# Mixing two batches ahead, a sum without turned rows, and expert weights kept in SBUF

## The chip, the core and the metric

The kernel runs on one core of one Trainium2 chip. The metric is device time in microseconds, as the median of several runs. The core's engines are TensorE (PE, with its weight loads as PEld), VectorE (DVE), ScalarE (ACT), GpSimd (POOL) and SyncE (SP), which here issues only DMAs. The engines run their own instruction streams and meet by semaphores. SBUF is the working memory, PSUM holds the products of TensorE, and DRAM holds inputs, outputs and rows that are dispatched by index.

## What is computed

A decoder of four layers on x (4 batches of 512 rows, 128 wide, fp32) with a context of 77 rows a batch. Each of twelve blocks is `x = layernorm(x + block(x))`. The change touches three of them:

```python
# layer 0, third block: mixing
x_prev = rows of x shifted down by one
xr = mu_r * x + (1 - mu_r) * x_prev
xk = mu_k * x + (1 - mu_k) * x_prev
out = sigmoid(xr @ W_r.T) * (square(relu(xk @ W_k.T)) @ W_v.T)

# layer 1, second block: sum with the context's mean
out = x1 @ W1.T + mean over the 77 rows of (x2 @ W2.T) + b

# layer 3, third block: experts (8 experts, each row goes to its best 2)
shared = (silu(x @ sw1) * (x @ sw3)) @ sw2
rw, sel = top_k(x @ router_w.T + experts_bias, 2);  rw = softmax(rw)
out = shared + sum over the 2 chosen e of rw * ((silu(x @ w1[e]) * (x @ w3[e])) @ w2[e])
```

## The kernel before

The twelve blocks run as a chain of stages. `Core.stage` opens a block of the five engines' streams; its end is a barrier, so no engine begins a stage before all have ended the one before. X holds the rows in their natural order, R the sums before the norm, and XT the rows turned (features on partitions), which most stages need as an operand of TensorE. The norm of a batch is written in four steps that several stages share: `norm_stats` on VectorE adds the block's result to X and takes mean and variance (L122, L125, L128), `norm_gpsimd` takes the power -1/2 on GpSimd (L160, L162) in two halves of a batch, `norm_apply` on VectorE scales into X (L143), and `norm_tensor` with `norm_scalar` turns X on TensorE (L170) and copies it into XT on ScalarE (L177).

**Mixing stage, `mixing_ffn`.** Per batch b of four: ScalarE makes two scaled copies of the shifted rows (`scale`, L1553), VectorE adds mu times x to them (`mix`, L1584 and L1588), TensorE multiplies (`first`, L1512 for k and L1517 for r), ScalarE takes relu and sigmoid (L1563, L1567), VectorE squares the relu (L1598), TensorE multiplies again (`second`, L1526), and VectorE forms the gated product Y (L1603). All buffers have two slots. The order on every engine is written by hand: `scale`, `mix` and `first` run one batch ahead, and `norm_apply` and the turning of batch b - 1 stand within batch b.

**Context stage, `context_sum`.** VectorE sums the context's rows (L1649) and spreads the mean of each batch over 128 columns (L1652). TensorE adds three products for each of 16 groups of rows (L1628 to L1630). The norm follows, and at the end X is turned into XT. The stage that follows, `experts_one`, normalises X once more and turns the result into XT on its own.

**Last stage, `experts_two`.** SyncE first writes X to rows in DRAM (L2907). TensorE and VectorE compute the routing; VectorE then makes a table `expert_i` that holds for each of 39 tiles of 128 rows the expert's number times 128, and the lists of row numbers. GpSimd issues for each tile an indirect gather of its rows into XG (L331, eight slots) and an indirect scatter of its results out of O (L335, four slots): first eight gathers, then for each tile a scatter and, while there are tiles left, a gather. TensorE turns a tile's rows (`turn`, L2951), multiplies with the expert's w1 and w3 (`up`, L2959) and w2 (`down`, L2967). ScalarE copies the turned rows (`take`, L3034) and applies silu (`gate`, L3040); VectorE forms the product (L3108) and copies the result into O (L3114). The orders are by hand: TensorE runs turn(i + 2), up(i + 1), down(i); ScalarE runs gate(i), take(i + 2). The shared expert's work is strewn between the tiles (L2931, L2932, L2943, L3028, L3075, L3080). The weights of a tile's expert, 128 x 768 fp32, are read from DRAM for every tile into WB (four slots) by SyncE:

```python
sp.wait_ge(found, 1)
for i in range(T):
    e = sp.value_load(disp.expert_i[0:1, i:i + 1], min_val=0, max_val=7 * P)
    if i >= RING:
        sp.wait_ge(o_ready, i - RING + 1)
    sp.dma_start(WB[:, i % RING, :], weights[bass.ds(e, P), :]).then_inc(loaded[i % RING], 16)
```

After the loop the results are read back, weighted, added and normalised, and written to the output.

## Time and profile before

| | |
|---|---|
| median of 3 runs | 2083.51 us (2081.59 to 2091.36) |
| profiled execution, its own time | 2109.39 us |
| span of its profile | 2107.5 us |
| PE busy | 1716.1 us (81%) |
| DVE busy | 1422.6 us (68%) |
| ACT busy | 1075.5 us (51%) |
| POOL busy | 416.6 us (20%) |
| granted PE clock, mean | 0.916 |
| DMA | 132.29 MB, mean 63 GB/s |

Times are microseconds from the start of the span unless marked ns. L1512 is line 1512 of the kernel. In a row of a timeline the first number is the start, the second the time covered, then engine, line, operation, output and inputs with their shapes, the count, and in brackets the idle time of the engine before it with what ended it. A row of several instructions covers them with the gaps between. The chain of waits is followed back from the last instruction; a piece named "another core or an unknown queue" is one for which the profile shows no releaser. Ends of matmuls are modelled.

### The profile page before, as it was taken

How to read it: one execution, taken by the hardware profiler on the slowest of the kernel's cores; microseconds unless marked ns; L12 is line 12 of the kernel's file. 1: busy time of each engine (PE TensorE's matmuls, PEld its weight loads, DVE VectorE, ACT ScalarE, POOL GpSimd, SP SyncE). 2: the span in 40 equal slices, each digit the busy share in tenths (PEclk: the TensorE clock that was granted, in tenths of full speed). 3: DMA queues.
4: the chain of work that ended last, by engine and by line, in shares of the span. 5: the costliest groups of instructions: out<-in, count | busy, mean ns of one | idle time of the engine just before them, and what ended most of it. 6: DMA issues, size and time to landing. Idle time of an engine off the chain costs nothing. (4 is left out here: it accounts for less than half of the span.)

```text
span 2107.5 us, 33370 instructions
## 1 busy us (share of the span) xinstructions
PE 1716.1 (81%) x11732; PEld 1022.0 (48%) x11822; DVE 1422.6 (68%) x3275; ACT 1075.5 (51%) x2294; POOL 416.6 (20%) x576
## 2 busy tenths in 40 slices
PE   4779858999977999985789999973699988796773
PEld 3546533333365666663644444432345444464662
DVE  4546578888764776765666767767699999575224
ACT  3346526777723445444455565543477777463221
POOL 0110030000032666652200000001200000100654
PEclk8999889999978999997999999995699999997896
DMA  4000000000025888861000000000000000001454
GB/s 121 1 1 2 1 1 0 1 1 1 1 94 199 315 327 324 334 238 42 1 1 0 1 1 1 1 1 18 1 1 2 2 1 1 1 2 51 136 156 129
DMA packets 42862, 132.29 MB, mean 63 GB/s; under 512 B 7106, under 2 KB 22635, under 8 KB 37611
## 3 DMA queue, kind: packets, MB, share of 16 engines
q1 hardware_dynamic: 32523, 116.98, 15.9%
q0 software_dynamic: 4992, 10.23, 1.5%
q10 hardware_dynamic: 5184, 2.95, 0.5%
q8 instruction: 97, 1.59, 0.3%
q14 instruction: 66, 0.54, 0.1%
HBM read 120.27 MB, written 14.58 MB: 64 GB/s over the span
## 5 line engine op out<-in xcount | busy, mean ns | idle before, releaser
L160 POOL TENSOR_SCALAR rstd<-MV 128x2 f32<-128x2 f32 (+1 forms) x100 | 27.0, 270 | 1014.6 <-DVE MV L128 1008.9
L855 DVE TENSOR_REDUCE l1aM<-PS 128x2 f32<-128x1024 f32 x128 | 152.9, 1220 | 22.6 <-PE PS L611 20.5
L773 ACT ACTIVATE l1aE<-PS 128x512 f32<-128x512 f32 x256 | 140.8, 595 | 48.7 <-PE PS L640 45.4
L773 ACT ACTIVATE l3aE<-PS 128x512 f32<-128x512 f32 (+3 forms) x256 | 102.5, 442 | 47.6 <-PE PS L644 44.8
L855 DVE TENSOR_REDUCE l3aM<-PS 128x2 f32<-128x256 f32 (+3 forms) x128 | 101.3, 819 | 20.7 <-PE PS L613 19.6
L2748 ACT COPY PT<-PS 128x512 f32<-128x512 f32 x128 | 68.9, 590 | 87.7 <-PE PS L2659 87.4
L2838 DVE TENSOR_REDUCE M<-PS 128x1 f32<-128x589 f32 x128 | 92.4, 764 | 24.0 <-PE PS L2648 23.7
L1879 PE MATMUL PS<-WB,H 128*128 128x512 f32 x234 | 107.7, 597 | 0.0
L2754 ACT ACTIVATE E<-PS,M 128x589 f32<-128x589 f32 x128 | 95.9, 763 | 19.4 <-DVE M L2838 19.3
L883 DVE SCALAR_TENSOR_TENSOR l3aE<-l3aE,l3aLB 128x2048 f32<-128x2048 f32 (+1 forms) x64 | 94.9, 1483 | 2.7 <-ACT l3aE L773 2.7
L611 PE MATMUL PS<-l1aKS,l1aQS 128*128 128x512 bf16 x249 | 76.8, 388 | 16.2 <-DVE l1aQS L878 5.5
L2019 ACT ACTIVATE H<-PS,WB 128x128 f32<-128x128 f32 x156 | 44.6, 368 | 89.0 <-DVE H L2158 58.5
L640 PE MATMUL PS<-l1aQS,l1aKS 128*128 128x512 bf16 x239 | 82.3, 387 | 5.2 <-ACT l1aE L773 4.0
L2676 PE MATMUL PS<-PT,Va 128*64 128x512 f32 x320 | 82.1, 611 | 0.8 <-ACT Q L2759 0.8
L2659 PEld LDWEIGHTS PS<-cols_const_sb,E 128*128 128x128 f32 x512 | 56.4, 141 | 47.2 <-DVE E L2858 31.5
L162 POOL TENSOR_TENSOR rstd<-rstd,mhalf 128x2 f32<-128x2 f32 (+1 forms) x100 | 77.4, 774 | 8.3
L640 PE MATMUL PS<-l3aQS,l3aKS 128*128 128x512 bf16 (+3 forms) x254 | 70.6, 307 | 3.4 <-ACT l3aE L773 2.0
L2032 ACT ACTIVATE A<-PS,WB 128x128 f32<-128x128 f32 x156 | 58.7, 457 | 27.9 <-PE PS L1889 27.9
L2648 PE MATMUL PS<-K,Q 64*128 64x512 f32 x256 | 72.3, 641 | 0.0
L2659 PE MATMUL PS<-cols_const_sb,E 128*128 128x128 f32 x512 | 69.2, 278 | 2.8 <-DVE E L2858 2.6
L611 PE MATMUL PS<-l3aKS,l3aQS 128*128 128x256 bf16 (+3 forms) x248 | 63.7, 309 | 8.8 <-DVE l3aM L855 5.6
L2858 DVE TENSOR_SCALAR E<-E,sums 128x589 f32<-128x589 f32 x128 | 67.6, 528 | 4.5
(686 smaller groups left out, 4488.2 us busy)
## 6 DMA issues: line engine op xcount, KB each, us to landing
WB<-in_experts SPq DMA_DIRECT2D x39, 1286.0 KB
TB<-mixed_tails SPq DMA_DIRECT2D x39, 768.5 KB
WB<-in_experts SPq DMA_DIRECT2D x39, 384.0 KB
mixed_tails<-in_tails SPq DMA_DIRECT2D x1, 2305.5 KB, 12.2
cols_fold_sb<-in_cols_fold SPq DMA_DIRECT2D x1, 1676.0 KB, 12.1
mixed_tails<-in_tails SPq DMA_DIRECT2D x1, 1537.0 KB, 16.1
mixed_tails<-WB SPq DMA_DIRECT2D x2, 768.5 KB, 4.2
cols_l2x_sb<-in_cols_l2x SPq DMA_DIRECT2D x1, 1154.0 KB, 9.1
```

Of the source, the lines that this page charges most:

```text
L162: g.tensor_tensor(out, out, self.mhalf[:, 0:out.shape[1]], ALU.pow).then_inc(done, 1)
L611: ins = mm(o, QS[:, pp, qt * P:(qt + 1) * P], keys(m)[:, pp, par, 0:kc], start=True, stop=not causal)
L640: ins = mm(o, keys(m)[:, pp, par, k0:k0 + kn], QS[:, pp, q0:S], start=True, stop=not (mask or causal))
L773: nc.scalar.activation(E[0:kn, home(m, kt) + j, q0:S], PS[0:kn, 4 + n % 2, q0:S], ACT.Exp, scale=SCALE).then_inc(exp_done, 1)
L855: v.tensor_reduce(M[:, m % 2, qt, 2 * hp:2 * hp + 2], PS[:, bank:bank + 2, 0:kc], AX, ALU.max, negate=True).then_inc(pair_free, 1)
L883: v.scalar_tensor_tensor(e, e, 1.0, LB[:, m % 2, :, kt * P:S], ALU.min, ALU.max).then_inc(clipped, 1)
L1879: mm(o, H1[:, i % 3, c * P:(c + 1) * P], mid_w(i, c), start=False, stop=False)
L2648: ins = mm(PS[:, at_ + 2 * par, :], Q[own, b % 2, pp, q], K[own, b % 2, pp, :], start=True, stop=True)
L2659: ins = nc.tensor.transpose(PS[:, at_ + 2 * par, t * P:(t + 1) * P], E[:, ring(x, par), e0:e0 + P], k.ident)
L2676: ins = mm(PS[64 * par:64 * par + 64, 6, :], Va[:, b % 2, t, h * DH:(h + 1) * DH], PT[:, n % 2, par, t, :], start=(t == 0), stop=(t == len ...
L2754: nc.scalar.activation(E[:, i, 0:NK], scores(s, par), ACT.Exp, bias=M[:, i:i + 1], accum_out=sums[:, i:i + 1]).then_inc(exp_done, 1)
L2838: ins = v.tensor_reduce(M[:, i:i + 1], scores(s, par), AX, ALU.max, negate=True)
```

## The change

- `mixing_ffn` runs `scale`, `mix` and `first` two batches ahead instead of one. The square of the relu moves from VectorE to ScalarE, directly behind the relu. `norm_apply` of a batch stands directly behind its statistics. The context's sum and mean are made here, between mix(1) and the first batch, in two buffers that are passed on.
- `context_sum` takes the mean from there. It no longer turns X into XT.
- `experts_two` reads the weights of all eight experts into a buffer ALL of 128 x 6144 fp32 at the start of the stage. ScalarE reads the expert's number of tile i and copies that expert's 768 columns from ALL into WB, two tiles ahead. SyncE has no part in the loop.

```diff
--- before.py
+++ after.py
@@ -1485,7 +1485,7 @@
                     "turned", "temp_abs", "decay_in", "xt_made", "shell_rooted"], body)
-def mixing_ffn(k, w):
+def mixing_ffn(k, w, cs, cr):
     nc, PS = k.nc, k.PS
@@ -1527,12 +1527,13 @@
                 ins.then_inc(kv_ready, 1)
             first(0)
+            first(1)
             for b in range(BT):
-                if b + 1 < BT:
-                    first(b + 1)
                 second(b)
                 if b:
                     k.norm_tensor(pe, normed, turned, b - 1, b - 1)
+                if b + 2 < BT:
+                    first(b + 2)
             k.norm_tensor(pe, normed, turned, BT - 1, BT - 1)
         @block.gpsimd
@@ -1553,14 +1554,17 @@
                     nc.scalar.mul(tmp[:, q, i, :], k.XT[:, b, 0:S], om[:, i:i + 1]).then_inc(scaled, 1)
             scale(0)
+            scale(1)
             for b in range(BT):
                 q = b % 2
-                if b + 1 < BT:
-                    scale(b + 1)
                 act.wait_ge(k_ready, b + 1)
+                nc.scalar.activation(kr[:, q, :], PS[:, q, :], ACT.Relu).then_inc(rectified, 1)
+                act.wait_ge(rectified, b + 1)
                 if b >= 2:
-                    act.wait_ge(acted, b - 1)
-                nc.scalar.activation(kr[:, q, :], PS[:, q, :], ACT.Relu).then_inc(rectified, 1)
+                    act.wait_ge(kv_ready, b - 1)
+                nc.scalar.activation(ka[:, q, :], kr[:, q, :], ACT.Square).then_inc(acted, 1)
+                if b + 2 < BT:
+                    scale(b + 2)
                 act.wait_ge(r_ready, b + 1)
                 if b >= 2:
                     act.wait_ge(gated_done, b - 1)
@@ -1588,68 +1592,53 @@
                 v.scalar_tensor_tensor(xr[:, q, :], k.xt(b), w["mu"][:, 0:1], tmp[:, q, 0, :], ALU.mult, ALU.add).then_inc(mixed_r, 1)
             mix(0)
+            mix(1)
+            step(v.tensor_reduce(cs[:, :], k.CT[:, :, :], AX, ALU.add))
+            step.wait()
+            for b in range(BT):
+                step(v.tensor_scalar(cr[:, b, :], k.ones, cs[:, b:b + 1], 1.0 / SC, ALU.mult, ALU.mult))
             for b in range(BT):
                 q = b % 2
-                if b + 1 < BT:
-                    mix(b + 1)
-                dve.wait_ge(rectified, b + 1)
-                if b >= 2:
-                    dve.wait_ge(kv_ready, b - 1)
-                v.tensor_tensor(ka[:, q, :], kr[:, q, :], kr[:, q, :], ALU.mult).then_inc(acted, 1)
-                if b:
-                    k.norm_apply(dve, normed, b - 1, b - 1)
+                if b + 2 < BT:
+                    mix(b + 2)
                 dve.wait_ge(gated, b + 1)
                 dve.wait_ge(kv_ready, b + 1)
                 v.tensor_tensor(Y[:, q, :], PS[:, 6 + q, :], r[:, q, :], ALU.mult).then_inc(gated_done, 1)
                 dve.wait_ge(gated_done, b + 1)
                 k.norm_stats(dve, Y[:, q, :].rearrange("p (t d) -> p t d", t=NT), step, b)
-            k.norm_apply(dve, normed, BT - 1, BT - 1)
+                k.norm_apply(dve, normed, b, b)
     k.stage("l0f", ["scaled", "mixed_r", "mixed_k", "r_ready", "k_ready", "rectified", "gated", "acted", "kv_ready", "gated_done",
                     "steps", "normed", "turned", "om_made"], body)
-def context_sum(k, w):
+def context_sum(k, w, cr):
     nc, PS = k.nc, k.PS
-    def body(block, summed, out_ready, steps, normed, turned):
-        cs = k.sb("ctx_sum", [P, BT])
-        cr = k.sb("ctx_mean", [P, BT, P])
+    def body(block, out_ready, steps, normed):
         @block.tensor
         def _(pe):
             mm = nc.tensor.matmul
             pe.wait_ge(w["landed"], 16)
             for b in range(BT):
-                pe.wait_ge(summed, b + 1)
                 for t in range(NT):
                     o = PS[:, 4 + b, t * P:(t + 1) * P]
                     mm(o, k.xt(b)[:, t * P:(t + 1) * P], w["w1"], start=True, stop=False)
                     mm(o, cr[:, b, :], w["w2"], start=False, stop=False)
                     ins = mm(o, k.ones_b, k.bias["l1x_b"], start=False, stop=True)
                 ins.then_inc(out_ready, 1)
-            for b in range(BT):
-                k.norm_tensor(pe, normed, turned, b, b)
         @block.gpsimd
         def _(pool):
             for b in range(BT):
                 k.norm_gpsimd(pool, b, b)
-        @block.scalar
-        def _(act):
-            for b in range(BT):
-                k.norm_scalar(act, turned, b, b)
-
         @block.vector
         def _(dve):
             v = nc.vector
             step = Count(dve, steps)
-            step(v.tensor_reduce(cs[:, :], k.CT[:, :, :], AX, ALU.add))
-            step.wait()
-            for b in range(BT):
-                v.tensor_scalar(cr[:, b, :], k.ones, cs[:, b:b + 1], 1.0 / SC, ALU.mult, ALU.mult).then_inc(summed, 1)
             for b in range(BT):
                 dve.wait_ge(out_ready, b + 1)
                 k.norm_stats(dve, PS[:, 4 + b, :].rearrange("p (t d) -> p t d", t=NT), step, b)
@@ -1657,7 +1646,7 @@
                     k.norm_apply(dve, normed, b - 1, b - 1)
             k.norm_apply(dve, normed, BT - 1, BT - 1)
-    k.stage("l1x", ["summed", "out_ready", "steps", "normed", "turned"], body)
+    k.stage("l1x", ["out_ready", "steps", "normed"], body)
 def experts_one(k, w, d, weights, tails, tails_made, bias_rows, bias_in, fold, rows, placed, gathered, scattered, ahead):
@@ -2884,8 +2873,8 @@
     def body(block, routed, lg_copied, pair_spread, exped, g_ready, silued, eo_done, d_ready, y_done, steps, normed, stored,
              marked, counted, found, tiled, spread, lowered, listed, known, rows_out, x_turned, x_taken, gu_ready, gate_done,
-             h_done, o_ready, o_taken, paired, weighed, added, *rings):
-        back, loaded = rings[0:RING], rings[RING:]
+             h_done, o_ready, o_taken, paired, weighed, added, all_in, loaded, *rings):
+        back = rings
         SG = k.sb("SG", [P, S])
         EO = k.sb("EO", [P, 2, S])
         lg = k.sb("logits", [P, N, 8])
@@ -2894,6 +2883,7 @@
         ixf = k.sb("best_at_f4", [P, N, 8])
         pw = k.sb("pair_w", [P, 4, N])
         WB = k.sb("WB3", [P, RING, 768])
+        ALL = k.sb("ALL3", [P, 8 * 6 * P])
         XG = k.sb("XG3", [P, XRING, P])
         XGT = k.sb("XGT3", [P, 2, P])
         HG = k.sb("HG", [P, 2, 2 * P])
@@ -2905,12 +2895,9 @@
         @block.sync
         def _(sp):
             sp.dma_start(rows.rearrange("(n p) d -> p n d", p=P), k.X[:, :, :]).then_inc(rows_out, 16)
-            sp.wait_ge(found, 1)
-            for i in range(T):
-                e = sp.value_load(disp.expert_i[0:1, i:i + 1], min_val=0, max_val=7 * P)
-                if i >= RING:
-                    sp.wait_ge(o_ready, i - RING + 1)
-                sp.dma_start(WB[:, i % RING, :], weights[bass.ds(e, P), :]).then_inc(loaded[i % RING], 16)
+            for e in range(8):
+                sp.dma_start(ALL[:, e * 6 * P:(e + 1) * 6 * P], weights[e * P:(e + 1) * P, :]).then_inc(all_in, 16)
+            sp.wait_ge(o_taken, T)
             for j in range(RING):
                 sp.wait_ge(scattered[j], 16 * len(range(j, T, RING)))
             for b in range(BT):
@@ -2951,7 +2938,7 @@
                 nc.tensor.transpose(PS[:, 6, 0:P], XG[:, i % XRING, :], k.ident).then_inc(x_turned, 1)
             def up(i):
-                pe.wait_ge(loaded[i % RING], 16 * (i // RING + 1))
+                pe.wait_ge(loaded, i + 1)
                 pe.wait_ge(x_taken, i + 1)
                 if i >= 2:
                     pe.wait_ge(h_done, i - 1)
@@ -3043,12 +3030,23 @@
             disp.spread_scalar(act, tiled, lowered)
             act.wait_ge(pair_spread, 1)
             nc.scalar.activation(pw[:, 1, :], pw[:, 0, :], ACT.Exp).then_inc(exped, 1)
+            def choose(i):
+                e = act.value_load(disp.expert_i[0:1, i:i + 1], min_val=0, max_val=7 * P)
+                if i >= RING:
+                    act.wait_ge(o_ready, i - RING + 1)
+                nc.scalar.copy(WB[:, i % RING, :], ALL[:, bass.ds(e * 6, 6 * P)]).then_inc(loaded, 1)
+
+            act.wait_ge(found, 1)
+            act.wait_ge(all_in, 128)
+            choose(0)
+            choose(1)
             take(0)
             take(1)
             for i in range(T):
                 gate(i)
                 if i + 2 < T:
                     take(i + 2)
+                    choose(i + 2)
                 if i in between and i and between[i][0] == "up":
                     shared_gate(*between[i][1:])
             for j in range(RING):
@@ -3152,7 +3150,7 @@
     k.stage("l3f", ["routed", "lg_copied", "pair_spread", "exped", "g_ready", "silued", "eo_done", "d_ready", "y_done", "steps", "normed",
                     "stored", "marked", "counted", "found", "tiled", "spread", "lowered", "listed", "known", "rows_out", "x_turned",
                     "x_taken", "gu_ready", "gate_done", "h_done", "o_ready", "o_taken", "paired", "weighed", "added",
-                    *(f"{s}{j}" for s in ("back", "loaded") for j in range(RING))], body)
+                    "all_in", "loaded", *(f"back{j}" for j in range(BT))], body)
 def quantised_ffn(k, w, ahead):
@@ -3566,9 +3564,11 @@
             k.stage("setup", ["bias_landed", "high_made", "middle_made", "low_made", "bias_split", "zeroed", "steps", "turned"], setup)
             charge_attention(k, W["l0a"], finish_constants)
             cross_attention(k, "l0x", W["l0x"], mask_b[:, :, :])
-            mixing_ffn(k, W["l0f"])
+            ctx_sum = one.enter_context(nc.sbuf_tensor("ctx_sum", [P, BT], F32))
+            ctx_mean = one.enter_context(nc.sbuf_tensor("ctx_mean", [P, BT, P], F32))
+            mixing_ffn(k, W["l0f"], ctx_sum, ctx_mean)
             attention16(k, "l1a", W["l1a"])
-            context_sum(k, W["l1x"])
+            context_sum(k, W["l1x"], ctx_mean)
         with ExitStack() as two:
             second = ["l2a", "l2x"]
```

## Rows read from the trace of the kernel before

**Rows 1.** Timeline of the mixing stage, VectorE and ScalarE: start, length, operation, idle before.

```profile
262.83 0.69 DVE L1603 TENSOR_TENSOR Y<-PS,r_gate 128x512 f32<-128x512 f32 x1 [2.96 <-PE PS L1526]
...
283.18 0.68 DVE L1603 TENSOR_TENSOR Y<-PS,r_gate 128x512 f32<-128x512 f32 x1
...
287.46 0.60 DVE L143 TENSOR_SCALAR X<-R,MV,rstd 128x128 f32<-128x128 f32 x2 [0.43 <-POOL rstd L162]
...
288.64 0.37 ACT L177 COPY XT<-PS 128x256 f32<-128x256 f32 x1 [0.68 <-PE PS L170]
```

**Rows 2.** Timeline of the context stage, its head and its tail.

```profile
594.84 0.47 DVE L1649 TENSOR_REDUCE ctx_sum<-CT 128x4 f32<-128x308 f32 x1 [1.46 <-PEq L87]
595.35 0.88 DVE L1652 TENSOR_SCALAR ctx_mean<-cols_const_sb,ctx_sum 128x128 f32<-128x128 f32 x4
...
595.78 0.76 PE L1628 MATMUL PS<-cols_l1x_sb,XT 128*128 128x128 f32 x2 [1.88 <-DVE ctx_mean L1652]
...
611.76 2.11 DVE L143 TENSOR_SCALAR X<-R,MV,rstd 128x128 f32<-128x128 f32 x8
...
614.07 0.89 ACT L177 COPY XT<-PS 128x256 f32<-128x256 f32 x2 [0.27 <-PE PS L170]
```

**Rows 3.** Timeline of GpSimd in the last stage's loop, scatters.

```profile
1960.47 1.01 POOL L335 DMA_INDIRECT expert_out<-O,l3f_to  x1 [0.41 <-issue]
...
1965.55 1.00 POOL L335 DMA_INDIRECT expert_out<-O,l3f_to  x1 [2.79 <-DVE O L3114]
...
1968.13 0.99 POOL L335 DMA_INDIRECT expert_out<-O,l3f_to  x1 [0.30 <-issue]
...
2076.92 0.97 POOL L335 DMA_INDIRECT expert_out<-O,l3f_to  x1 [0.30 <-issue]
```

**Rows 4.** Groups by line, 1950 to 2077: busy us, mean ns, idle before and releasers.

```profile
L3040 ACT ACTIVATE HG<-PS 128x256 f32<-128x256 f32 x39 | 15.0, 385 | 35.0 <-PE PS L2959 22.2 <-DMA WB<-mixed_out 8.1 <-issue 4.8
L3034 ACT COPY XGT<-PS 128x128 f32<-128x128 f32 x39 | 10.4, 267 | 49.8 <-PE PS L2951 27.2 <-DMA WB<-mixed_out 19.5 <-issue 3.1
...
L2959 PE MATMUL PS<-XGT,WB 128*128 128x128 f32 x312 | 47.7, 302 | 2.6 <-DMA WB<-in_experts 2.5
```

**Rows 5.** Chain of waits from 1870 on: start, length, what.

```profile
1968.37 5.85 another core or an unknown queue
...
1975.47 3.72 DMA WB<-in_experts
```

**Rows 6.** Timeline of TensorE and ScalarE, 1969 to 1976, one tile turned and taken.

```profile
1970.02 0.27 PE L2951 MATMUL PS<-cols_const_sb,XG 128*128 128x128 f32 x1
...
1974.28 0.27 ACT L3034 COPY XGT<-PS 128x128 f32<-128x128 f32 x1 [4.00 <-DMA WB<-mixed_out]
```

**Rows 7.** The page: bandwidth in 40 equal slices of the span, 52.7 us each.

```profile
GB/s 121 1 1 2 1 1 0 1 1 1 1 94 199 315 327 324 334 238 42 1 1 0 1 1 1 1 1 18 1 1 2 2 1 1 1 2 51 136 156 129
```

**Rows 8.** Timeline of ScalarE at the mixing stage's start.

```profile
254.81 2.56 ACT L1553 ACTIVATE tmp<-XT,one_minus_mu 128x512 f32<-128x512 f32 x4 [0.51 <-DVE one_minus_mu L1577]
```

**Rows 9.** Groups by line, 254.3 to 289.1: one of the two mixes.

```profile
L1588 DVE SCALAR_TENSOR_TENSOR xr<-XT,cols_l0f_sb,tmp 128x512 f32<-128x512 f32 x4 | 3.0, 744 | 0.0
```

**Rows 10.** Timeline of ScalarE in the first attention stage; L1339 is a Square.

```profile
64.44 1.76 ACT L3552 ACTIVATE gather<-terms 128x768 bf16<-128x768 f32 x2
66.10 0.37 ACT L1339 ACTIVATE shell_sq<-PS 128x256 f32<-128x256 f32 x1
66.49 1.28 ACT L1342 ACT_TABLE_LOAD   x1
```

**Rows 11.** SyncE's register instructions per tile: ns min/median/max, first and last start.

```profile
L2910 SPq TENSOR_LOAD <-l3f_expert_i x39: 78/268/710, 1938.1 to 2068.5; - x39
L2910 SPq FUSED_REGOPS  x39: 3/152/159, 1938.5 to 2068.8; - x39
L2910 SPq SEQ_ASSERT  x39: 2/18/442, 1938.7 to 2069.0; - x39
```

**Rows 12.** Who waited for whom, ScalarE, 690 to 950: total us, times, longest.

```profile
ACT H L2019 <- remote: 2.2, 1, 2.2
```

## Prediction

> **What bounds the kernel now.** The program is a chain of stages, each ended by a barrier, so every stage that ends earlier moves all that follows. I read the bandwidth row of the page first, then the timelines of the three stages that the diff touches, and for the last of them the groups by line, the chain of waits and SyncE's instructions.
>
> The mixing stage (254.6 to 289.0 us) is bound by VectorE. From its first gated product at 262.83 until its last normalised row at 287.46 + 0.60 = 288.06 VectorE rarely stops, and then one turn and one copy of 0.37 follow, to 289.01 [rows 1]. The context stage (594.8 to 615.0) has a head in which TensorE waits for the context's mean, a middle paced by VectorE, and a tail in which the last rows are turned and copied [rows 2].
>
> The last expert stage holds a loop of 39 tiles. Its first scatter stands at 1960.47, its last at 2076.92, 116.5 us later [rows 3]. In steady stretches GpSimd issues a scatter every 2.58 us (1965.55 and 1968.13, with a gather between), and that is its own queue, not a wait. 31 steps with a gather each at 2.58, then seven scatters alone at about 1.28, make 1960.5 + 80.0 + 9.0 = 2049.4; I add two because the last tiles go at TensorE's pace. A queue that never starved would end at 2051; this one ends 26 us later. The reader should see that TensorE waits for weights only little in name (2.5 us in the group of the up products), while the chain has transfers of weights (3.72 us at 1975.47) and long pieces whose releaser it can't name (5.85 us at 1968.37) [rows 4, 5]. One of these in detail: TensorE turned a tile at 1970.02, in 0.27 us, and ScalarE took it at 1974.28, 4.0 us late [rows 6]. No tensor that it needs was missing. All along, the loop moves 136 to 156 GB/s [rows 7], three quarters of it weights: 39 times 384 KB against 8 times.
>
> **The profiled run and the median.** The profiled execution took 2109.4 us (span 2107.5, 1.9 around it), the median of the timed runs is 2083.5, 25.9 us less. The unnamed stalls are about as large as that gap. I can't tell from one trace whether they belong to the kernel or to being profiled; this is the largest unknown of the sum.
>
> **Mixing stage.** Removed from VectorE: four squares of k_relu, each a 512-column operation between two of its batches. They go to ScalarE, where a 512-column operation from SBUF costs 2.56 / 4 = 0.64 us [rows 8]. Moved: the mixes of batches 2 and 3 run ahead of the gated products. Added: a reduction of 0.47 and four means of together 0.88 us [rows 2], placed after mix 1. They are covered by the 2.96 us that VectorE stands before 262.83 [rows 1]; with mix 2 (two instructions of 0.744, [rows 9]) that makes 2.84 us, which just fits. If the cover were gone, it would be up to 1.4 us.
>
> Added waits: VectorE now applies the norm of a batch right behind its statistics, so it waits for GpSimd's two powers. The last batch of before has just that order: 283.18 to 288.06 = 4.88 us from the product to the last row [rows 1]. Queued behind that wait are mix 3 and the next product. ScalarE gets two scales (1.28 us) and one square (0.64) ahead of its first sigmoid, and the table load of 1.28 [rows 10] comes behind them: the sigmoid ends near 263.0 instead of 261.1. The first product waits for it and starts at 263.05 instead of 262.83. From there VectorE: four batches at 4.88 and one mix of 1.49 give 263.05 + 19.5 + 1.5 = 284.1, against 288.06. Bounds: if TensorE's second product of batches 2 and 3 or ScalarE's copies come late, a microsecond each is lost; if the waits for GpSimd are shorter, half a microsecond is won. I take 4.0 us (2.0 to 4.8).
>
> Square needs no table of its own as far as the trace shows: at 66.10 it follows a scaling at 64.44 with no load between, and the load of 1.28 us comes only behind it, for the next function [rows 10]. So it ran under a table that was not made for it. The trace has no square next to a sigmoid. The Trainium skill ("ScalarE: Activation LUTs", section on table sets) names relu, copy, identity and abs as members of every set, not square; by that the two could lie in different sets. That is a rival below.
>
> **Context stage.** Removed at the head: TensorE starts at 595.78 because it waits for the mean; VectorE's first instruction is at 594.84, so TensorE can start 0.9 us earlier. Removed at the tail: VectorE's last rows end at 611.76 + 2.11 = 613.87, the last copy at 614.07 + 0.89 = 614.96 [rows 2]: 1.1 us. The next stage turns its own rows and doesn't read these. Late next is VectorE, which is busy throughout. I take 2.0 us (1.5 to 2.1).
>
> **Last stage.** Removed: 39 transfers of weights on SyncE's queue, each behind a register read. Added: eight transfers (3.1 MB) behind the copy of the rows to DRAM, at the stage's start, some 28 us before the first gather; at the 156 GB/s of rows 7 they take 20 us, so they are covered. ScalarE waits for all of them and for the routing, then chooses two tiles before it takes the first; all of that is over before the first gather lands. Its price there is nothing; if instruction or row transfers were delayed by the burst, up to 3 us.
>
> Added in the loop, on ScalarE, per tile: a register read and a copy of 768 columns. Two operations of 768 columns from SBUF took 1.76 us on ScalarE [rows 10], so 0.88 each. The register path by SyncE's rows is 0.27 + 0.15 + 0.02 us at the medians and 0.71 + 0.16 + 0.44 at the maxima [rows 11]; ScalarE has no such row, so I take 0.5 to 1.4 us, the gaps between them included. ScalarE's own work is 0.385 + 0.267 us [rows 4], and the seven shared gates of 0.6 add 0.1 a tile. A tile then costs ScalarE 2.15 us at the low end and 3.05 at the high end, against GpSimd's 2.58. I take the low end, because a register path is short while ScalarE still computes the operation ahead of it. Behind it in ScalarE's queue are the next gate and the shared gate, and VectorE and TensorE wait for those; the ring of four O tiles and eight gathers absorbs that while the mean stays under 2.58.
>
> The Trainium skill ("DMA: Bandwidth & Descriptors", section on latency and other measured facts) gives a register load a floor of about 600 ns. The rows here show a median of 268 ns, so the measurement decides. By the Trainium skill's figure ScalarE would need some 2.5 us a tile, which leaves the sum as it is.
>
> What it brings: at most the 26 us by which the loop exceeds its queue, at least nothing. If the whole gap between profile and median lies in this loop, the timed loop already ends as if at 2051 and nothing is left. With none of the gap there, up to 26 are left. The part with a name, transfers of weights on the chain (3.72 us in the one shown), speaks for a real gain. I take 9 us.
>
> **The sum.** On the profiled execution: 2109.4 - 4.0 - 2.0 - 17 = 2086 if two thirds of the stalls go. For the median I count only 9 us of the last: 2083.5 - 15.0 = 2068.5, forecast 2069.
>
> **Rivals.**
> 1. The queue already paces the timed loop: the stalls were the profile's. For it speaks the equality of 26 and 25.9 us, and the earlier expert loop, which moves over 300 GB/s [rows 7] and has a single unnamed wait of ScalarE of 2.2 us [rows 12]. Against it: a transfer of weights stands on the chain. Gain 6 to 10 us in all: 2073.5 to 2078.
> 2. All the stalls were the weights' transfers: 2083.5 - 6 - 26 = 2051.5, with leftovers up to 2060.
> 3. Slower: ScalarE becomes the bound of the loop. It can begin when the first tile is turned, four us after the first gather, near 1954, and 3 us pass from its last gate to the last scatter. At 3.05 us a tile the loop ends at 1957 + 39 x 3.05 = 2076, against a queue that would have ended at 2051: +25 - 6 = +19, so 2102.5. It decides the sign by over 0.5% from 2.83 us a tile on (+16.4 in the loop). At 2.75 us it ends at 2064 and the result is 2090.5.
> 4. Square and sigmoid in different tables: two loads of 1.28 us a batch. ScalarE then needs about 6.4 us a batch and bounds the mixing stage, whose gain falls from 4 to about 0: 2072.5 with all else as forecast. Its price is from rows 10.
>
> **Chances.** Forecast (2062 to 2073) 0.43; rival 1 0.25; rival 2 0.15; rival 3 0.10 for the slow end and 0.04 for the mild one; rival 4 0.03. About 0.5% (10.4 us) is what a measurement of this kernel tells from no change, so faster means under 2073.1. Forecast, rival 2 and two thirds of rival 4 are faster: 0.60. Rival 1, the mild end of 3 and the rest of 4 are the same: 0.30. Slower 0.10. The range leaves out half of rival 2 and the slow end of 3: 2055 to 2090.
>
> **What would show it.** Mixing stage: product to last row 4.9 us in each batch, end near 285, one table load. Context stage: TensorE starts with VectorE's slot, no copies at the end. Loop: scatters 2.58 us apart nearly throughout, no waits of ScalarE without a releaser, under 80 GB/s. The prediction is wrong if stalls of 3 to 4 us remain though weights no longer move, if the copy takes over 1.0 us, or if ScalarE's instructions stand back to back at more than 2.6 us a tile.

## The result and the profile after

The changed kernel takes 2078.8 us (median of 21 runs, 2071.0 to 2083.8) against 2089.6 us (21 runs, 2081.2 to 2099.2) for the kernel before, run beside each other: a ratio of 0.9946, 95% interval 0.9935 to 0.9957, or 11.3 us less. The forecast was 2069, its range 2055 to 2090. So it is faster, by just over the 0.5% named in the prediction, and by three quarters of what was forecast. The forecast stood on 2083.5 us, the median of the first three runs of before; over 21 runs that median is 2089.6. Of the 9.8 us between forecast and result 6.1 are this shift. The profiled run of after took 2078.8 us (span 2076.9), exactly the median.

The mixing stage, which answers to [rows 1], [rows 8] and [rows 9]. Timeline of VectorE and ScalarE in the kernel after: start, length, engine, operation, idle before and what ended it.

```profile
258.08 0.47 DVE L1596 TENSOR_REDUCE ctx_sum<-CT 128x4 f32<-128x308 f32 x1
...
259.03 0.63 ACT L1565 ACTIVATE k_act<-k_relu 128x512 f32<-128x512 f32 x1
...
260.90 1.28 ACT L1571 ACT_TABLE_LOAD   x1
262.20 0.60 ACT L1571 ACTIVATE r_gate<-PS 128x512 f32<-128x512 f32 x1
...
262.89 0.69 DVE L1606 TENSOR_TENSOR Y<-PS,r_gate 128x512 f32<-128x512 f32 x1 [1.10 <-ACT r_gate L1571]
...
273.86 0.68 DVE L1606 TENSOR_TENSOR Y<-PS,r_gate 128x512 f32<-128x512 f32 x1
...
278.65 0.68 DVE L1606 TENSOR_TENSOR Y<-PS,r_gate 128x512 f32<-128x512 f32 x1
...
282.92 0.60 DVE L143 TENSOR_SCALAR X<-R,MV,rstd 128x128 f32<-128x128 f32 x2 [0.43 <-POOL rstd L162]
...
284.11 0.37 ACT L177 COPY XT<-PS 128x256 f32<-128x256 f32 x1 [0.66 <-PE PS L170]
```

One table load, the first product at 262.89, the third and the last 4.79 us apart, from product to last row 282.92 + 0.60 - 278.65 = 4.87 us. The stage runs from 254.46 to 284.48, 30.0 us against 34.4.

The context stage, which answers to [rows 2]: timeline of TensorE's start and VectorE's end. No copies follow; the next stage's first instruction is the last line.

```profile
589.42 0.77 PE L1628 MATMUL PS<-cols_l1x_sb,XT 128*128 128x128 f32 x2 [0.93 <-PEq L87]
...
605.31 2.11 DVE L143 TENSOR_SCALAR X<-R,MV,rstd 128x128 f32<-128x128 f32 x8
607.74 0.87 DVE L2061 BATCH_NORM_STATS2 S<-X 128x6 f32<-128x128 f32 x4 [0.32 <-PEq L87]
```

The last stage's loop, which answers to [rows 3] and [rows 4]: timeline of GpSimd's scatters near the end, and then the groups by line from 1950 to 2077.

```profile
2035.15 0.99 POOL L335 DMA_INDIRECT expert_out<-O,l3f_to  x1 [0.31 <-issue]
2037.72 0.99 POOL L335 DMA_INDIRECT expert_out<-O,l3f_to  x1 [0.30 <-issue]
2039.01 0.98 POOL L335 DMA_INDIRECT expert_out<-O,l3f_to  x1 [0.30 <-issue]
...
2046.66 0.97 POOL L335 DMA_INDIRECT expert_out<-O,l3f_to  x1 [0.30 <-issue]
```

```profile
L3037 ACT COPY WB<-ALL 128x768 f32 x37 | 30.8, 832 | 11.6 <-issue 11.6
...
L3021 ACT COPY XGT<-PS 128x128 f32<-128x128 f32 x39 | 10.3, 265 | 21.8 <-PE PS L2938 21.8
```

The last scatter stands at 2046.66, 89.4 us after the first, against 116.5 in the profile of before. ScalarE's wait for a turned tile is 21.8 us, all with TensorE's name; the 19.5 us of [rows 4] under a transfer's name are gone, and so are the unnamed pieces of [rows 5]. Bandwidth as in [rows 7]:

```profile
GB/s 123 1 1 2 1 1 1 1 1 1 1 92 217 311 327 325 331 253 42 1 0 1 1 1 1 1 1 18 0 1 2 1 1 2 1 2 7 101 52 85
```

Read alone, the two profiles say that the loop gave 27 us and the early stages 6.4. But their spans differ by 30.6 us and the medians by 10.8. A profile of before that stands 20 us above its own median can't be set against one of after that stands on it. That is what the experiments were for.

### The profile page after: what moved, and what is told of

It reads as the page before. It is cut to its first block and busy times, and to the rows that moved or that the text cites. A ratio compares the mean times of both kernels' runs of the same rounds, so it can differ in the third digit from the quotient of the medians.

```text
span 2076.9 us, 33295 instructions
## 1 busy us (share of the span) xinstructions
PE 1713.3 (82%) x11716; PEld 1018.4 (49%) x11806; DVE 1420.7 (68%) x3271; ACT 1103.9 (53%) x2329; POOL 412.8 (20%) x576
## 5 line engine op out<-in xcount | busy, mean ns | idle before, releaser
L855 DVE TENSOR_REDUCE l3aM<-PS 128x2 f32<-128x256 f32 (+3 forms) x128 | 101.1, 818 | 18.8 <-PE PS L613 17.7
L2008 ACT ACTIVATE H<-PS,WB 128x128 f32<-128x128 f32 x156 | 44.5, 368 | 89.3 <-PE PS L1856 89.2
L2665 PE MATMUL PS<-PT,Va 128*64 128x512 f32 x320 | 82.8, 616 | 0.8 <-ACT Q L2748 0.8
```

What stands on the lines that cost most here:

```text
L855: v.tensor_reduce(M[:, m % 2, qt, 2 * hp:2 * hp + 2], PS[:, bank:bank + 2, 0:kc], AX, ALU.max, negate=True).then_inc(pair_free, 1)
L2665: ins = mm(PS[64 * par:64 * par + 64, 6, :], Va[:, b % 2, t, h * DH:(h + 1) * DH], PT[:, n % 2, par, t, :], start=(t == 0), stop=(t == len ...
```

## The experiments

Two chips took part. On the first, where before_again, experts_only, early_only and second_copy ran, the kernel before takes 2113.7 us. On the other it takes 2090.1 and 2089.8 us, as in the measurement of the result (2089.6), for which no chip is on record. All runs on the first chip are of one sitting, so something that passes would look the same as a property of the chip. "Loop" is the time from the first scatter of the last stage to its last. Each ratio is against runs of before on the same chip, with its 95% interval; it can differ by 0.1 to 0.2% from that of the two medians.

### Which part of the change pays

**before_again**: no edit.

> The kernel before, unchanged, as a control and for a second profile. The profile of before that the prediction used took 2109.4 us, some 20 us above that kernel's own median of 2089.6 us, and its tile loop ran 126.8 us from the first scatter's end of the chain to the last. Theory A (the tile loop's stalls come from the weight transfers, and the timed runs carry a few of them, 5 us or so): a profile nearer to the median shows the loop at 100 to 107 us, with scatters 2.57 us apart except for a few gaps that no instruction's work explains. Theory B (the timed runs of before are paced by GpSimd's queue alone, all stalls were that one run's): the loop takes 99 to 101 us, and the 5 us of the 11.3 that the two early stages do not explain come from elsewhere. Ratio to before: 1.000 within 0.002 by both.

Measured: 2114.1 us, ratio 0.9989 (0.9967 to 1.001). Loop 110.3 us, more than either theory allowed: both took this run to be near 2089.6 us. The 126.8 us in the expectation are not the loop of the first profile, which is 116.5 us [rows 3].

**experts_only**: the kernel before with the last stage of after.

```diff
-                sp.dma_start(WB[:, i % RING, :], weights[bass.ds(e, P), :]).then_inc(loaded[i % RING], 16)
+            for e in range(8):
+                sp.dma_start(ALL[:, e * 6 * P:(e + 1) * 6 * P], weights[e * P:(e + 1) * P, :]).then_inc(all_in, 16)
...
+                nc.scalar.copy(WB[:, i % RING, :], ALL[:, bass.ds(e * 6, 6 * P)]).then_inc(loaded, 1)
```

> Only the last stage's edit: the eight experts' weights are loaded once and copied per tile by ScalarE; mixing stage and context stage as before. Theory A (per-tile weight transfers stall GpSimd's queue or the tiles in timed runs too): the median falls by 3 to 8 us (ratio 0.996 to 0.9985), and the scatters are 2.57 us apart throughout. Theory B (the queue already paces before's timed loop): ratio 1.000 within 0.001, unless the later stages took from elsewhere. By the sum, experts_only and early_only together should give the whole -11.3 us.

Measured: 2114.6 us, ratio 0.9997 (0.9979 to 1.0015). Loop 108.3 us, without weight transfers. The ratio is theory B's; its interval ends at a gain of 4.4 us and leaves no room for the forecast 9.

**early_only**: the kernel after with the last stage of before, the same diff the other way round.

> Only the mixing stage's and the context stage's edit: two batches ahead, the square on ScalarE, the mean made in the mixing stage, no rows turned in the context stage; the tile loop with its per-tile weight loads as before. The two profiles give 4.4 us for the mixing stage and 2.0 us for the context stage. Theory A: -6.4 us, ratio 0.997, and the profile shows the mixing stage at 30.0 us and the context stage at 18.4 us. Theory B (the 5 us left over are an after-effect of the early edits, not of the loop): -11 us, ratio 0.9945.

Measured: 2100.4 us, ratio 0.9922 (0.9894 to 0.995). Loop 109.5 us with the weight transfers.

The last stage's edit gives nothing that can be measured here, and the two early edits give 13 us by the medians (16.5 by the ratio, 11 to 22), more than the 6.4 of the two traces. Both were against theory A, on which the forecast of the loop rested. And the stalls stand in experts_only as well, in a loop with no weights on the move. The waits of ScalarE for a tile turned by TensorE, in the timelines of before_again (first fence) and experts_only:

```profile
1981.22 0.27 PE L2951 MATMUL PS<-cols_const_sb,XG 128*128 128x128 f32 x1
...
1985.42 0.29 DVE L3114 COPY O<-PS 128x128 f32<-128x128 f32 x1 [3.49 <-remote]
1985.45 0.27 ACT L3034 COPY XGT<-PS 128x128 f32<-128x128 f32 x1 [3.98 <-DMA WB<-mixed_out]
1985.56 1.42 SPq L2913 DMA_DIRECT2D WB<-in_experts  x2
```

```profile
2005.24 0.27 PE L2949 MATMUL PS<-cols_const_sb,XG 128*128 128x128 f32 x1
...
2008.55 0.27 ACT L3032 COPY XGT<-PS 128x128 f32<-128x128 f32 x1 [3.25 <-DMA WB<-mixed_out]
```

These are the lines of [rows 6]. The reader should see that the transfer named as releaser can't be one of weights: experts_only has none left. Nor was it one in [rows 4] and [rows 6]: in the trace of before the last WB<-mixed_out is issued at 951.5 us, a thousand us ahead of the loop. In before_again VectorE, ScalarE and SyncE, each of which waits for TensorE, go on within 0.14 us of each other. That speaks for a TensorE that stood still and whose recorded ends, which are modelled, come too early; it is not shown.

The stalls can be counted: the takes that come more than 1 us after the recorded end of their turn with ScalarE idle. Of 39 there are 9 in before, 6 in before_again, 6 in experts_only, 10 in early_only and 5 in second_copy, the longest 1.5 to 4.0 us. In the nine profiles that were taken on the other chip or with the result there is none, and the longest is 0.04 us. So the profile that the prediction used has the mark of the first chip. By the prediction's own sign (stalls of 3 to 4 us though weights no longer move) its reading of the loop was wrong.

**after_again**: no edit, on the other chip.

> The changed kernel again. On the chip of the four runs before it, the last stage's edit alone gave nothing (0.9997) and the two early stages' edits alone 0.9922. Theory C (the whole gain of the change comes from the two early stages, and the tile loop is not moved in timed runs): ratio 0.992 to 0.995. Theory A' (the tile loop's edit pays only where TensorE does not pause): if the loop of this profile again takes 89 to 92 us from the first scatter to the last (89.4 in the profile of after, against 108 to 111 in the four others), the pauses belong to the chip or the run; if it takes 108 to 110 us on the same chip as the other four, the 89.4 us were the chip's.

Measured: 2078.6 us, ratio 0.9936 (0.9914 to 0.9957). Loop 89.5 us. The ratio is theory C's. The loop is short again, but the chip and the last stage's edit both differ from early_only's 109.5 us; early_again tells them apart.

**early_again**: early_only, on the other chip.

> The two early stages' edits without the last stage's, once more, for the chip on which the changed kernel gave 0.9936 in the same call and the tile loop takes 89 us with and without per-tile weight loads. Theory C (the last stage's edit is worth nothing): the same ratio as the whole change, 0.9925 to 0.995. Rival (the eight loads at the head of the last stage and ScalarE's copies cost a little): up to 2 us faster than the changed kernel, 0.991 to 0.9935.

Measured: 2078.5 us, ratio 0.9939 (0.9925 to 0.9952). Loop 89.3 us.

With and without the last edit the time is the same (2078.6 and 2078.5 us), and so is the loop. The stretch from the first to the last scatter, busy time of PE, PEld, DVE, ACT and POOL, granted clock, DMA share and GB/s, of mixing_only (a transfer of weights per tile), after (none), early_only (a transfer per tile) and experts_only (none); the last two on the first chip:

```profile
1955.80:2044.90 89.10, 78.15 (x571) 66.71 (x570) 32.10 (x89) 26.19 (x79) 67.50 (x69) 1.00 0.71 207
```

```profile
1957.30:2046.70 89.40, 79.54 (x570) 68.27 (x569) 31.35 (x89) 52.57 (x115) 67.49 (x70) 0.98 0.19 52
```

```profile
1959.00:2068.50 109.50, 84.73 (x569) 70.22 (x567) 32.06 (x89) 25.40 (x79) 67.49 (x70) 0.97 0.55 168
```

```profile
1974.60:2083.00 108.40, 89.43 (x563) 76.29 (x562) 31.20 (x89) 52.67 (x115) 67.48 (x70) 0.89 0.16 42
```

207 or 52 GB/s: 89 us. 168 or 42 GB/s: 109 us. The transfers don't matter, the chip does. The clock isn't it either: early_only has 0.97 and 109.5 us. What holds up the takes of TensorE's results for 1 to 4 us on the first chip was not found (see the end). The kernel before itself has no profile on the other chip; mixing_only and context_only, each with its last stage, stand for it.

### The early stages

**mixing_only**: the kernel before with after's mixing stage, without the mean.

```diff
             first(0)
+            first(1)
             for b in range(BT):
...
+                nc.scalar.activation(ka[:, q, :], kr[:, q, :], ACT.Square).then_inc(acted, 1)
...
-                v.tensor_tensor(ka[:, q, :], kr[:, q, :], kr[:, q, :], ALU.mult).then_inc(acted, 1)
...
+                k.norm_apply(dve, normed, b, b)
```

> Only the mixing stage's edit (two batches ahead, the square on ScalarE), without the mean; context stage and tile loop as before. The traces give the stage 34.7 us before and 30.3 to 30.6 us with the edit: 4.1 us. Theory C1 (the stage's own saving is all): ratio 0.998. Theory C2 (the saving moves where the later stages fall in TensorE's stretches at half clock, and these give the rest of the 13 us of early_only): ratio 0.994 to 0.997. The profile's tile loop with per-tile weight loads also tells what that loop takes on this chip: 109 to 111 us as in the profiles so far, or 90 to 100 us if the pauses are the chip's.

Measured: 2079.5 us, ratio 0.9944 (0.9923 to 0.9965). Loop 89.1 us. The ratio is in theory C2's range. Alone it gives about as much as the whole change.

**context_only**: before's mixing order and square, the mean added behind mix 0, after's context stage, before's last stage.

```diff
             mix(0)
+            step(v.tensor_reduce(cs[:, :], k.CT[:, :, :], AX, ALU.add))
+            step.wait()
+            for b in range(BT):
+                step(v.tensor_scalar(cr[:, b, :], k.ones, cs[:, b:b + 1], 1.0 / SC, ALU.mult, ALU.mult))
...
-            for b in range(BT):
-                k.norm_tensor(pe, normed, turned, b, b)
```

> Only the context stage's edit (the mean made by VectorE in the mixing stage, no rows turned); the mixing stage's order and VectorE's square as before, the tile loop as before. The traces give 20.4 to 19.7 us before and 17.7 to 18.3 us with the edit: 2.0 to 2.7 us, less what the mean costs in the mixing stage (0.47 + 4 x 0.1 us of VectorE's time ahead of its second mix, at most 1 us). Theory C1: ratio 0.9985 to 0.9995. Theory C2: 0.996 to 0.998. With mixing_only it should add up to early_only's 0.9922 (0.989 to 0.995).

Measured: 2084.6 us, ratio 0.9969 (0.9952 to 0.9985). Loop 89.2 us. The ratio is in theory C2's range. The two single edits add up to 18 us by their ratios, the pair gives 13 in early_again; the intervals (7 to 16 and 3 to 10 us) allow that.

**vector_square**: early_only with the square on VectorE, ahead of the mix.

```diff
-                nc.scalar.activation(ka[:, q, :], kr[:, q, :], ACT.Square).then_inc(acted, 1)
...
+                v.tensor_tensor(ka[:, q, :], kr[:, q, :], kr[:, q, :], ALU.mult).then_inc(acted, 1)
                 if b + 2 < BT:
                     mix(b + 2)
```

> early_only with the square back on VectorE, ahead of the mix two batches on: it tells the order (two ahead) from the engine of the square. The prediction put 4.88 us per batch from product to last row with the square on ScalarE and VectorE as the bound of the stage. If VectorE's load sets the stage, the square's 0.7 us comes back four times: 33 us against 30.6. If the order alone gave the gain, it stays at 30.6. Expected by the prediction's steps: 32.5 to 33.5 us, ratio to before 0.993 to 0.996.

Measured: 2080.0 us, ratio 0.995 (0.9931 to 0.9969), as expected. The stage takes 36.8 us in the profile, not 32.5 to 33.5.

**one_ahead**: early_only with the square on ScalarE and before's order.

```diff
-                if b + 2 < BT:
-                    mix(b + 2)
+                if b + 1 < BT:
+                    mix(b + 1)
+                if b:
+                    k.norm_apply(dve, normed, b - 1, b - 1)
```

> early_only with the mixing stage's old order (one batch ahead, rows' scaling deferred) and the square on ScalarE: the fourth corner beside before (old order, VectorE), vector_square (new order, VectorE: 36.8 us for the stage) and early_only (new order, ScalarE: 30.6 us). If the square's engine gives the gain, the stage takes 31 to 33 us here; if it needs both, 34 to 38 us, as before.

Measured: 2084.4 us, ratio 0.9975 (0.9957 to 0.9993). The stage takes 37.4 us, as expected if it needs both.

The lengths of the stages in all profiles, from each stage's first instruction in its trace to the next stage's (us):

| profiles | mixing | attention | context | the three |
|---|---|---|---|---|
| before | 34.7 | 305.5 | 20.4 | 360.6 |
| before_again | 38.5 | 304.3 | 19.7 | 362.4 |
| experts_only | 34.7 | 305.6 | 20.4 | 360.7 |
| context_only | 38.5 | 304.2 | 18.2 | 360.8 |
| one_ahead | 37.4 | 301.3 | 18.5 | 357.2 |
| vector_square | 36.8 | 304.6 | 18.4 | 359.8 |
| mixing_only | 30.5 | 301.4 | 20.0 | 351.9 |
| after | 30.3 | 304.6 | 18.3 | 353.3 |
| after_again, early_only, early_again, second_copy | 30.6 | 302.8 | 17.7 | 351.1 |
| second_copy_2, half_gathers | 30.6 | 301.3 | 18.4 | 350.3 |

The three profiles with both old stages have a mean of 361.2 us, the seven with both new ones 351.2. These 10.0 us are nearly the whole 11.3. They aren't the chip's: on the first chip alone early_only and second_copy have 351.1. The old mixing stage takes 34.7 or 38.5 us, the new one 30.3 to 30.6 in every profile. Why, stands in the gated products. Timeline of VectorE: before_again's third and fourth (compare 278.04 in the profile of before, where the third waited 0.52), and early_again's last three.

```profile
281.44 0.69 DVE L1603 TENSOR_TENSOR Y<-PS,r_gate 128x512 f32<-128x512 f32 x1 [3.36 <-PE PS L1526]
...
287.32 0.69 DVE L1603 TENSOR_TENSOR Y<-PS,r_gate 128x512 f32<-128x512 f32 x1 [0.65 <-PE PS L1526]
```

```profile
269.99 0.68 DVE L1606 TENSOR_TENSOR Y<-PS,r_gate 128x512 f32<-128x512 f32 x1
...
274.77 0.68 DVE L1606 TENSOR_TENSOR Y<-PS,r_gate 128x512 f32<-128x512 f32 x1
...
279.56 0.68 DVE L1606 TENSOR_TENSOR Y<-PS,r_gate 128x512 f32<-128x512 f32 x1
```

Windows of both kernels from 274 to 284: before_again first, then early_again.

```profile
274.00:284.00 10.00, 6.12 (x22) 4.86 (x22) 6.44 (x22) 2.72 (x7) 3.15 (x6) 0.66 0.00 0
```

```profile
274.00:284.00 10.00, 4.67 (x18) 3.16 (x17) 8.18 (x31) 3.12 (x8) 4.04 (x9) 0.55 0.00 0
```

In the old order the product of nearly every batch waits for TensorE's second product of the same batch. When TensorE falls to its lower level, 1.2 of 2.4 GHz, in the middle of the stage, that wait grows from 0.5 to 3.4 us. In the new order TensorE has a batch of lead, and at a granted clock of 0.55, lower still, VectorE doesn't wait and is busy 8.2 of 10 us. The profile of before happened to have 1.00 in this stretch and so showed the smaller of the two savings.

vector_square has the waits again, 0.91 to 2.24 us in each batch, and one_ahead 2.8 and 3.7 us in its first three: the traces say that it takes both the order and the square's engine. The times show the order alone: one_ahead's interval lies above early_again's (0.9925 to 0.9952). vector_square's overlaps it, 1.5 us apart in the medians, though its profile has the stage 6 us longer. That profile is of its slowest run (2084.4 us), so the square's engine is not shown to matter in most runs.

### What paces the loop

**second_copy** and **second_copy_2**: after with one more copy per tile, on the first and on the other chip.

```diff
+        SPARE = k.sb("SPARE3", [P, RING, 768])
...
+                nc.scalar.copy(SPARE[:, i % RING, :], ALL[:, bass.ds(e * 6, 6 * P)])
                 nc.scalar.copy(WB[:, i % RING, :], ALL[:, bass.ds(e * 6, 6 * P)]).then_inc(loaded, 1)
```

> The changed kernel with a second 768-column copy per tile on ScalarE into a buffer that nobody reads: 39 x 0.83 us more work on ScalarE in the loop, about 1.8 + 0.83 = 2.65 us per tile against GpSimd's 2.57. Theory A (ScalarE had 0.75 us per tile of room and the loop is paced by GpSimd's queue): ScalarE becomes the bound by a hair, the loop is 0 to 8 us longer than the changed kernel's, that is a ratio to before of 0.995 to 0.9985. Rival (GpSimd's queue is not the pace, the tiles wait on the latency from ScalarE's copy through TensorE and VectorE to the scatter): most of the added 32 us shows up, a ratio to before of 1.008 or more.

Measured: 2103.4 us, ratio 0.9944 (0.9925 to 0.9964). Loop 111.3 us. The rival's 1.008 is far off. That is 3.0 us above early_only; the kernel after without the second copy was not run on this chip.

> The changed kernel with a second 768-column copy per tile on ScalarE once more. Where TensorE pauses (first time) its loop took 111.3 us against 108.3 to 110.3. In a loop at GpSimd's pace of 2.57 us per tile (89.4 us for 38 intervals less the first eight, which have no gather beside them) ScalarE's 1.8 + 0.83 = 2.65 us per tile, and 0.6 more in every fourth, should now be the pace: 2.65 to 2.85 us per tile, a loop of 95 to 106 us, and the time 6 to 16 us above the changed kernel's. If the loop stays at 89 to 91 us, ScalarE's register path and copies overlap with its other work more than the sum says.

Measured: 2081.8 us, ratio 0.9953 (0.9937 to 0.9969), 3.3 us above after_again. Loop 94.6 us, a little under the 95 to 106 expected, and the time is under the expected 6 to 16 us too, so ScalarE's work overlaps more than that sum says.

**half_gathers**: after without every second gather; the odd tiles work on the rows of the tile before them.

```diff
-            for i in range(XRING):
+            for i in range(0, XRING, 2):
                 disp.gather(XG[:, i, :], i).then_inc(gathered[i], 16)
...
-                if i + XRING < T:
+                if i % 2 and i - 1 + XRING < T:
```

> The changed kernel with every second of the 39 gathers left out: the odd tile takes the rows of the even one before it, so its output rows are wrong ones. 19 of GpSimd's 78 indirect DMAs go, 19 x 1.28 = 24 us. Theory (GpSimd's queue is the pace of the loop): the four gathers fewer ahead of the first scatter give 5 us, and the loop falls from 89.4 us to the next bound, TensorE's 2.1 us per tile or ScalarE's 1.8 to 2.0: 70 to 82 us, a ratio of 0.982 to 0.99 to before. Rival (something else than the queue, such as the latency of a tile or the DMA writes, sets the 2.57 us): the loop stays over 86 us.

Measured: 2068.7 us, ratio 0.9891 (0.9871 to 0.991), 10 us under after_again. The ratio is as the theory has it, the loop of 82.7 us just over its 82, and under the rival's 86. Windows from the first to the last scatter (the same columns as above): half_gathers, then second_copy_2.

```profile
1955.20:2038.00 82.80, 77.94 (x573) 66.79 (x571) 30.97 (x89) 51.98 (x115) 53.00 (x55) 1.00 0.15 43
```

```profile
1954.80:2049.50 94.70, 80.19 (x571) 66.83 (x569) 30.49 (x89) 76.33 (x151) 67.51 (x70) 1.00 0.17 49
```

GpSimd's queue is the pace of the loop on the undisturbed chip: fewer gathers make it shorter, by 6.7 us from scatter to scatter, until TensorE is busy 77.9 of 82.8 us. That next bound is close behind, so most of the 24 us of gathers left out don't show. Nor do the 5 us expected ahead of the first scatter: it comes 38.1 us after the start of the stage here as in after, because it waits 5.28 us for the first tile's result. ScalarE could take 0.83 us a tile more for 5.2 us in all; after's one copy had room.

## Why the prediction was right, and where not

**Mixing stage, -4.0 (2.0 to 4.8).** The steps held within 0.6 us: sigmoid end 262.8 (forecast 263.0), first product 262.89 (263.05), 4.87 us from product to last row (4.88), VectorE's end 283.5 (284.1), the mean covered, one table load. The square took 0.63 us (0.64) and needed no table of its own, so rival 4 fell. Against this one profile the saving is 4.4 us. But the term was mis-sized: [rows 1] showed TensorE's waits at one course of the clock. In the three profiles with both old stages it takes (34.7 + 38.5 + 34.7) / 3 = 36.0 us, in the seven new ones 30.6: 5.4 us, and 7.9 where the clock falls at the wrong time. How often the timed runs take which course isn't known. The prediction called the stage bound by VectorE, which "rarely stops" from the first product on. It was wrong in that: the 2.96 us ahead of the first product in [rows 1] had TensorE's name, and in the timeline of before VectorE waits for TensorE ahead of the second product as well:

```profile
271.26 0.69 DVE L1603 TENSOR_TENSOR Y<-PS,r_gate 128x512 f32<-128x512 f32 x1 [2.44 <-PE PS L1526]
```

**Context stage, -2.0.** 20.4, 19.7 and 20.4 us became 17.7 to 18.4, on average 20.2 and 18.0: 2.2 us. TensorE started in the stage's first slot, and no copies follow.

**A term that was missing, in part by chance.** The attention stage between the two, which the diff doesn't touch, averages 305.1 us in the three profiles with both old stages and 302.6 in the seven new ones: 2.5 us less. In before_again the 36.6 us from its start have a granted clock of 0.69, in early_again 0.77:

```profile
293.40:330.00 36.60, 25.88 (x81) 10.14 (x84) 27.07 (x29) 12.89 (x20) 8.07 (x4) 0.69 0.00 0
```

```profile
285.50:322.10 36.60, 24.86 (x88) 9.57 (x91) 28.11 (x30) 14.11 (x23) 8.07 (x4) 0.77 0.00 0
```

In all fourteen profiles the length goes with this clock: at 0.69 or 0.70 the stage takes 304.2 to 305.6 us, at 0.77 it takes 301.3 to 302.8. But the change doesn't settle which: the profile of after has 0.69 and 304.6 us, and one_ahead, with the old order and a mixing stage of 37.4 us, has 0.77 and 301.3. So the 2.5 us are a mean over few profiles, and that the new mixing stage causes them is not shown.

**Last stage, -9 (0 to -26).** Wrong, and rival 1 was right: a queue that never starves was the right bound. From the first scatter on, 31 steps of 2.58 and seven of 1.28 are 89.0 us, and the loop on the other chip meets that (89.1 us with a transfer per tile, 89.4 without); the two us that the prediction added did not come. The step that failed is "The part with a name, transfers of weights on the chain (3.72 us in the one shown), speaks for a real gain". Without any transfer the loop takes 108.3 us on the first chip (110.3 with them) and 89.4 on the other (89.3 with them). So by these profiles the transfers cost 2 us at the most, not 9. And the stalls were not the profile's either, as rival 1 had it: they go with a chip. The profile of before, at 2109.4 us, lies in the band of the chip that has them (2105 to 2122), while the timed runs beside it (2082 to 2091) lie in the band of the other. The equality of 26 and 25.9 us, which the prediction weighed and set aside, was the right clue.

**ScalarE's price.** The copy took 0.832 us (0.88 forecast), the register path shows as 11.6 us of gaps before 37 copies, 0.31 each (0.5 forecast at the low end), so a tile costs 0.83 + 0.31 + 0.38 + 0.27 + 0.1 for the shared gates = 1.9 us instead of 2.15. Rival 3 was far off: second_copy_2 with 0.83 us more costs 3.3 us. The load itself, in after: ns min/median/max, first and last start.

```profile
L3034 ACTq TENSOR_LOAD <-l3f_expert_i x39: 272/278/472, 1938.7 to 2040.4; - x39
```

The Trainium skill ("DMA: Bandwidth & Descriptors", section on latency and other measured facts) gives a register load a floor of about 600 ns; the trace doesn't agree, with a median of 278 ns here and 268 in [rows 11]. The eight loads and the copies together cost nothing that could be measured: after_again against early_again is 0.1 us.

**The sum.** -4 - 2 - 9 = -15 was forecast; -5.4 - 2.2 - 2.5 + 0 = -10.1 is what the stages show, -11.3 (9.0 to 13.6) was timed. Faster came true without the term that was to carry most of it: two errors of opposite sign, 9 us too much in the loop and 4 too little ahead of it. That the sum came near is luck. The gain of 11.3 us lies a little above rival 1's 6 to 10, and the time of 2078.8 a little above its 2073.5 to 2078, which counted from 2083.5. By the prediction's own mark, under 2073.1, the time is not faster; against the 2089.6 beside it, it is.

**Open.** context_only was timed 6.5 us faster (3 to 10) with only 2 us visible in its stage, and one profile each can't say where the rest is. The stage behind it takes 357.3 us there, against 361.1 to 363.0 in the four profiles with the old context stage, but 356.8 to 362.3 in the others with the new one. The latent stage takes 378 us in three profiles and 381 to 384 in the others, among old and new kernels alike.

## What to carry to other kernels

Ahead of any sum, set the profiled run beside the median: where it stands 1% off, its stalls may be those of another chip, and one more profile of the unchanged kernel is worth more than any reasoning on them. A transfer on the chain of waits need not be a cost; what the loop would take at the pace of its fullest queue is the bound to compare with, and where the timed loop meets it, nothing feeding it can bring a gain. A stage that waits for TensorE can cost more than one profile shows, when the clock falls in it in other runs (34.7 and 38.5 us here); with a batch of lead for TensorE and less work on VectorE it took 30.3 to 30.6 us at any course of the clock seen.

## What was not expected of the hardware

- On one of two chips results of TensorE are taken late, in short pauses. In the last loop of before (the profile of [rows 3]), before_again, experts_only, early_only and second_copy ScalarE takes a turned tile 1 to 4 us after TensorE's recorded end, 5 to 10 times in 39 tiles, and the loop takes 108 to 117 us. In after, after_again, mixing_only, context_only, vector_square, early_again and one_ahead it takes 89.1 to 89.5 us. What pauses is open. It isn't the weights' traffic (experts_only, 42 GB/s) nor the granted clock (early_only, 0.97). The profile books these waits under a transfer or "another core or an unknown queue"; the transfer it names, WB<-mixed_out, doesn't exist in the loop of any of these kernels.
- The clock's course repeats. The old mixing stage took 34.7 us twice (before and experts_only, 1.00 from 274 to 284 us, with different last stages) and 38.5 us twice (before_again and context_only, 0.66, on different chips).
- 768 columns copied in ScalarE from SBUF to SBUF, with the source's offset from a register, take 0.83 us, and the register path ahead of it shows as a gap of 0.31 us.
